# Sums of the spectral products moved to VectorE, rotations finished in their outputs, and the even half's inverse one step earlier

## The reference, cut to what matters

```python
x = x + 0.5 * ffn(layernorm(x))          # 4 x 1024 x 256, fp32
x = x + ssm(layernorm(x))
x = x + 0.5 * ffn(layernorm(x))          # the same weights

def ffn(x):                              # weights are ternary, each layer has its scales
    h = silu((x @ w1.T) * w1_s) * ((x @ w2.T) * w2_s)     # 256 -> 1024
    h = gelu((h @ h1.T) * h1_s)                            # 1024 -> 1024
    h = gelu((h @ h2.T) * h2_s)                            # 1024 -> 1024
    return (h @ w3.T) * w3_s                               # 1024 -> 256

def ssm(x):                              # per channel: convolution over the 1024 tokens with K(log_dt, A, C)
    y = irfft(rfft(x, 2048) * rfft(K, 2048), 2048)[:1024]
    return gelu(y) @ W.T + b
```

## Time and profile before

| what | value |
|---|---|
| median of 3 runs | 1566.58 us (1562.31, 1566.58, 1566.74) |
| the profiled execution's own time | 1557.19 us |
| its span, first to last instruction | 1555.4 us |
| PE busy | 1481.7 us, 95% |
| DVE busy | 1059.9 us, 68% |
| ACT busy | 523.1 us, 34% |
| POOL busy | 265.2 us, 17% |
| mean granted TensorE clock | 0.985 |

### The profile page before, as it was taken

How to read it: one execution, slowest core, us unless ns; L and a number is a source line. 1 busy time by engine, 2 the same in 40 slices (tenths; PEclk the granted TensorE clock), 3 DMA queues, 4 the chain that set the end, 5 groups by cost and what they waited for, 6 DMA issues and landing times.

```text
span 1555.4 us, 17475 instructions
## 1 busy us (share of the span) xinstructions
PE 1481.7 (95%) x6912; PEld 1194.5 (77%) x6912; DVE 1059.9 (68%) x1691; ACT 523.1 (34%) x743; POOL 265.2 (17%) x245
## 2 busy tenths in 40 slices
PE   7698979989999999999999999999999999999998
PEld 3477867777777777878778787687887878888887
DVE  6697577977758777786778867687477775344432
ACT  5334235444442331423324232232322323232231
POOL 0024563735500002001021010210102100000000
PEclk9899999999999999999999999999999999999999
DMA  8100000000010412103121031220212211000000
GB/s 303 53 1 28 27 15 14 28 14 14 28 38 28 144 46 68 62 17 122 41 78 58 11 122 41 68 68 33 74 41 68 68 38 42 27 14 28 28 1 14
DMA packets 52258, 78.24 MB, mean 50 GB/s; under 512 B 2768, under 2 KB 44752, under 8 KB 50896
## 3 DMA queue, kind: packets, MB, share of 16 engines
q1 hardware_dynamic: 52176, 77.12, 14.7%
HBM read 56.14 MB, written 20.97 MB: 50 GB/s over the span
## 4 chain that ended last, share of the span: by engine, by line
PE 76%; DVE 10%; issue 8%; ACT 3%; POOL 2%; DMA 1%; DVEq 0%; POOLq 0%; ACTq 0%
PE ps L1291 59%; PE ps L1333 7%; PE ps L1370 3%; PE ps L1423 2%; PE ps L1340 2%; DVE hid_a_lo L1215 1%; ACT L620 1%; DVE hid_a_hi L1213 1%; DVE table L886 1%; ACT ph L620 1%; DMA ks<-k_d 1%; PE ps L1364 1%; PE ps L1365 1%; DVE table L879 1%; DVE tt L1018 1%
## 5 line engine op out<-in xcount | busy, mean ns | idle before, releaser
L577 ACT ACTIVATE act_o<-ps,scales 128x512 f32<-128x512 f32 x384 | 264.8, 690 | 962.2 <-PE ps L1291 958.4
L1291 PE MATMUL ps<-hid_a_hi,h 128*128 128x512 f32 x1024 | 409.6, 400 | 6.3 <-DVE hid_a_lo L1206 6.1
L1291 PE MATMUL ps<-hid_b_hi,h 128*128 128x512 f32 x1024 | 404.9, 395 | 0.8 <-DVE hid_b_lo L1215 0.7
L1291 PE MATMUL ps<-hid_a_lo,h 128*128 128x512 f32 x1024 | 404.2, 395 | 0.0
L1291 PE MATMUL ps<-hid_b_lo,h 128*128 128x512 f32 x1024 | 401.6, 392 | 0.0
L1291 PEld LDWEIGHTS ps<-hid_a_hi,h 128*128 128x128 f32 x1024 | 194.6, 190 | 55.0 <-issue 7.5
L1291 PEld LDWEIGHTS ps<-hid_a_lo,h 128*128 128x128 f32 x1024 | 194.5, 190 | 43.4 <-issue 2.2
L1291 PEld LDWEIGHTS ps<-hid_b_hi,h 128*128 128x128 f32 x1024 | 192.5, 188 | 45.2 <-DVE hid_b_lo L1215 2.1
L1291 PEld LDWEIGHTS ps<-hid_b_lo,h 128*128 128x128 f32 x1024 | 192.5, 188 | 42.9 <-issue 1.2
L1291 PE MATMUL ps<-hid_b_hi,w 128*128 128x512 f32 x480 | 189.9, 396 | 2.4 <-DVE gz L1268 2.1
L1291 PE MATMUL ps<-hid_b_lo,w 128*128 128x512 f32 x480 | 188.9, 394 | 0.0
(11 more groups left out here) (235 smaller groups left out, 1707.5 us busy)
## 6 DMA issues: line engine op xcount, KB each, us to landing
ks<-k_d SPq DMA_DIRECT2D x32, 512.0 KB, 4.2
stages<-in_weights SPq DMA_DIRECT2D x8, 1024.0 KB, 7.7
gz<-in_x SPq DMA_DIRECT2D x8, 512.0 KB, 3.9
xin<-in_x SPq DMA_DIRECT2D x8, 512.0 KB, 3.9
x_d<-xin SPq DMA_DIRECT2D x8, 512.0 KB, 2.9
z_d<-xin SPq DMA_DIRECT2D x8, 512.0 KB, 2.9
k_d<-ks SPq DMA_DIRECT2D x8, 512.0 KB, 2.9
zb<-z_d SPq DMA_DIRECT2D x8, 512.0 KB, 5.6
```

Of the source, the lines that this page charges most:

```text
L577: A(act_o[:, k % ACT_SLOTS], bank(source), func, scale=scale).then_inc(s_act, 1)
L1291: last = MM(o, weight[:, k, cols].bitcast(dt), part[:, k].bitcast(dt), start=(k == 0 and i == 0), stop=(k == n - 1 and i == len(act_) - 1))
```

## The change

It has four parts.

1. The sum of each product's halves is done by DVE right behind the product, in `products`. All products go to `tt`, so each product and its sum wait for one another on DVE. POOL's `sums`, its two gathering additions and their semaphore s_y are gone; a new DVE function `gather_even` writes their results to `tt` and signals s_pre. PE's `inverse_even` reads them there.
2. `rotate` first writes the sine products into its two outputs and then finishes them in place, so it does not use `tt`. `rotate_quarter` now issues its two sine products itself, at its own step; `fold_third` issues two instructions fewer.
3. In first tiles the even products come at k = 14 to 17 and `gather_even` at k = 18, `rotate_odd` at k = 18 and 19 (was 14, 15), `inverse_even` on PE before step 20 (was 21), on ACT at k = 20, on DVE at k = 21 and 22. ACT's `copy_even` is at k = 14 (was 16), writes to fb and no longer waits for `rotate_odd`; `scale_even` does.
4. In first tiles norm1 is at k = 11, 12 (was 18, 19) and norm2 at k = 19, 20 (was 20, 21). On POOL in second tiles the two additions of the bias come before norm2's inverse root (were behind it).

```diff
     if first_of(T):
-        return 18, 19
+        return 11, 12
...
@@ norm2_at
+    if first_of(T):
+        return (19, 20) if T <= TILES else (-1, -1)
     return (20, 21) if 4 < T <= TILES else (-1, -1)
...
@@ POOL
-            def sums(c, i):
-                pool.wait_ge(s_prod, (c - 1) * 8 + i + 1)
-                t = product_home(i)
-                G.tensor_tensor(fb[:, spectrum_at(i)], t[:, 0:4:2], t[:, 1:4:2], ALU.add).then_inc(s_y, 1)
...
-                if first:
-                    for i in range(4):
-                        sums(first, i)
-                    inverse_root("first", T + 1)
-                    pool.wait_ge(s_y, (first - 1) * 8 + 4)
-                    G.tensor_tensor(zb[:, 0:2], fb[:, 4:6], fb[:, 6:8], ALU.add)
-                    G.tensor_tensor(zb[:, 2:4], fb[:, 4:6], fb[:, 6:8], ALU.subtract).then_inc(s_pre, 1)
-                    if norm2_at(T)[0] >= 0:
-                        inverse_root("second", T - 1)
-                elif second:
-                    for i in range(4, 8):
-                        sums(second, i)
+                if second:
                     inverse_root("first", T + 1)
                     pool.wait_ge(s_xc, 32 * second)
                     pool.wait_ge(s_wt, 32 * second)
-                    if norm2_at(T)[0] >= 0:
-                        inverse_root("second", T - 1)
                     for g in range(2):
                         half = wb[:, g * J:(g + 1) * J]
                         last = G.tensor_tensor(half, half, bias.unsqueeze(1).to_broadcast([P, J, D]), ALU.add)
                     last.then_inc(s_bias, 1)
+                    if norm2_at(T)[0] >= 0:
+                        inverse_root("second", T - 1)
+                elif first:
+                    inverse_root("first", T + 1)
+                    if norm2_at(T)[0] >= 0:
+                        inverse_root("second", T - 1)
...
@@ ACT
             def copy_even(c):
-                act.wait_ge(s_rb, c + 1)
                 act.wait_ge(s_ef, c + 1)
-                A(zb[:, 0:2], units(7), ACT.Copy).then_inc(s_cpe, 1)
+                A(fb[:, 4:6], units(7), ACT.Copy).then_inc(s_cpe, 1)
...
             def scale_even(c):
                 act.wait_ge(s_ei, c)
+                act.wait_ge(s_rb, c + 1)
...
-                if first and k == 16:
+                if first and k == 14:
                     copy_even(first)
-                if first and k == 21:
+                if first and k == 20:
                     scale_even(first)
...
@@ DVE
+            def rotate(out0, out1, x0, x1, c_, s_):
+
+                V.tensor_scalar(out0, x1, s_, None, ALU.mult)
+                mark(V.tensor_scalar(out1, x0, s_, None, ALU.mult))
+                marked()
+                V.scalar_tensor_tensor(out0, x0, c_, out0, ALU.mult, ALU.subtract)
+                return V.scalar_tensor_tensor(out1, x1, c_, out1, ALU.mult, ALU.add)
...
@@ products
-                if i >= 2:
-                    dve.wait_ge(s_y, n - 1)
                 marked()
...
-                V.tensor_tensor(t, x, k_, ALU.mult).then_inc(s_prod, 1)
+                V.tensor_tensor(tt.rearrange("p (h u) d -> p h (u d)", h=2), x, k_, ALU.mult).then_inc(s_prod, 1)
+                dve.wait_ge(s_prod, n + 1)
+                mark(V.tensor_tensor(fb[:, spectrum_at(i)], tt[:, 0:4:2], tt[:, 1:4:2], ALU.add))
+
+            def gather_even():
+                marked()
+                V.tensor_tensor(tt[:, 0:2], fb[:, 4:6], fb[:, 6:8], ALU.add)
+                V.tensor_tensor(tt[:, 2:4], fb[:, 4:6], fb[:, 6:8], ALU.subtract).then_inc(s_pre, 1)
...
                     if k in (14, 15):
-                        rotate_odd(k - 14)
+                        products(first, k - 14)
                     if k == 16:
-                        products(first, 0)
-                        products(first, 1)
-                    if k == 17:
                         spectrum_even(first)
                         products(first, 2)
-                    if k == 18:
+                    if k == 17:
                         products(first, 3)
+                    if k == 18:
+                        gather_even()
+                    if k in (18, 19):
+                        rotate_odd(k - 18)
+                    if k == 21:
+                        inverse_even(first)
                     if k == 22:
-                        inverse_even(first)
-                    if k == 23:
                         inverse_even_again(first)
...
@@ PE
-                whole(6, C4, zb[:, 0:2])
-                whole(7, S4, zb[:, 2:4], s_ei)
+                whole(6, C4, tt[:, 0:2])
+                whole(7, S4, tt[:, 2:4], s_ei)
...
-                if first and k == 21:
+                if first and k == 20:
                     inverse_even(first)
```

More of the change, by code:

```diff
@@ L255, in build @@
             "s_of", "s_cpo", "s_ab", "s_oi", "s_sco", "s_inv", "s_yt", "s_tr", "s_g", "s_pj", "s_x2", "s_x2st"))
-        s_prod, s_y, s_pre, s_preo, s_wt, s_xc, s_bias = (sem(n) for n in (
-            "s_prod", "s_y", "s_pre", "s_preo", "s_wt", "s_xc", "s_bias"))
+        s_prod, s_pre, s_preo, s_wt, s_xc, s_bias = (sem(n) for n in (
+            "s_prod", "s_pre", "s_preo", "s_wt", "s_xc", "s_bias"))
         s_mir, s_l1k, s_turn, s_kfin = (sem(n) for n in ("s_mir", "s_l1k", "s_turn", "s_kfin"))
@@ L956, in rotate_odd @@
                 marked()
-                V.tensor_scalar(tt[:, 0:2], x1, col(C_S4), None, ALU.mult)
-                mark(V.tensor_scalar(tt[:, 2:4], x0, col(C_S4), None, ALU.mult))
-                marked()
-                last = rotate(wb[:, 4 * h:4 * h + 2], wb[:, 4 * h + 2:4 * h + 4], x0, x1, col(C_C4))
+                last = rotate(wb[:, 4 * h:4 * h + 2], wb[:, 4 * h + 2:4 * h + 4], x0, x1, col(C_C4), col(C_S4))
                 if h:
@@ L990, in turn @@
                     dve.wait_ge(s_ef, 1)
+                    dve.wait_ge(s_rb, 1)
                 if i >= 2:
@@ L1039, in gather_odd @@
             def gather_odd(c):
-                dve.wait_ge(s_y, c * 8)
+                marked()
                 V.tensor_tensor(wb[:, 0:4], fb[:, 0:4], fb[:, 4:8], ALU.add)
@@ L1063, in unrotate @@
                 marked()
-                V.tensor_scalar(tt[:, 0:2], x, col(C_SA + j), None, ALU.mult)
-                mark(V.tensor_scalar(tt[:, 2:4], y, col(C_SA + j), None, ALU.mult))
-                marked()
-                last = rotate(fb[:, j:j + 7:6], fb[:, 2 + j:5 + j:2], y, x, col(C_CA + j))
+                last = rotate(fb[:, j:j + 7:6], fb[:, 2 + j:5 + j:2], y, x, col(C_CA + j), col(C_SA + j))
                 if j:
@@ L1130, in spectral @@
                     if k in (14, 15):
-                        rotate_odd(k - 14)
+                        products(first, k - 14)
                     if k == 16:
-                        products(first, 0)
-                        products(first, 1)
-                    if k == 17:
                         spectrum_even(first)
                         products(first, 2)
+                    if k == 17:
+                        products(first, 3)
                     if k == 18:
-                        products(first, 3)
+                        gather_even()
[3 more added lines that the diff above has]
+                        inverse_even(first)
                     if k == 22:
-                        inverse_even(first)
-                    if k == 23:
                         inverse_even_again(first)
```

25 lines of the change are left out of this document (5 added, 20 removed).

## The result

The changed kernel takes 1535.62 us, the median of 4 runs (1533.72 to 1538.41); the kernel before, run beside it, 1564.44 (4 runs, 1558.42 to 1566.74). The ratio is 0.9824, 95% interval 0.9802 to 0.9847. The forecast was 1546.0 with a range of 1540 to 1554: the sign and the mechanism came true, the size is outside the range. The medians lie 28.8 us apart, the profiled executions less: 1555.4 us of span before, 1534.3 after, so 21.1 us, and the forecast said 20.6.

What follows compares the result with a forecast made beforehand. PE, busy 95% of the span, was taken as the bound; its wait and slow clock at the even inverse cost 21.2 us. Minus about 0.15 x 4 this gave 20.6, so 1566.6 - 20.6 = 1546.0 us, range 1540 to 1554.

Steps and rivals of the forecast that it cites:

- The wait and the clock behind it: PE at the even inverse of four first tiles: 12.7 us of wait, 8.5 of slow clock and restart.
- the ceiling: Most the change could win: wait and slow clock at the even inverse over four first tiles, 21.2 us.
- The first tile: First tiles were to last 92.3 to 93.0 us instead of 97.6, at clock 1.00.
- the part kept back: Remaining PE wait for s_pre at the even inverse, 0 to 0.3 us per first tile; about 0.15 x 4 deducted.
- DVE's chain: First tiles, k = 14 to 18: product-and-sum pairs of 1.9 us, s_pre at 791.1, 0.1 to 0.3 us of slack.
- The zeros: Parts costed at 0: rotate_odd's move, norm1 at k = 11 and 12, second tiles, bias order, T = 4.
- A: Rival: s_pre comes 0.5 to 2 us late at the even inverse; gain 11 to 17, 1550 to 1556 us; chance 0.11.
- B: Rival: an equal wait takes its place at scale_even or layer_three; no gain seen, 1562 to 1570 us; chance 0.06.
- C: Rival: late tap load for product 2 or 3 holds DVE's queue; slower, 1574 us at 8 us late; chance 0.04.
- the last move of the sum: The 20.6 us saving was taken from the median, 1566.6 to 1546.0, instead of the profiled execution, 1557.2 to 1536.6.

Runs made afterwards that it cites:

- second profile of before: The kernel before, unchanged, profiled again: 1559.88 us (span 1558.1), one run.
- the repeat of the changed kernel: The changed kernel as it is, run again beside the kernel before on chip 0: 1535.1 us (5 runs), ratio 0.9821.

## Why the prediction was wrong in size

By its own steps, the mechanism held. What failed is the baseline from which the saving was taken, and the saving itself was sized too small: 20.6 us, where T = 5 to 12 gave 23.5.
- **The wait and the clock behind it** are gone, 47.1 us of ACT's idle became 4 x 6.42 = 25.7: 21.4 us, where the ceiling was 21.2 and the forecast 20.6. The 0.15 us per tile kept back for a late s_pre was not needed: gather_even's last addition ends at 784.71, PE starts the inverse at 785.09.
- **The first tile** T = 7 came to 92.16 us; 92.3 to 93.0 was named, again without the part kept back.
- **DVE's chain** came true within 0.05 us at each point, with the measured cost of the wait between product and sum. The sum starts 0.03 us after its product's end (778.67 against 777.41 + 1.23), a split that waits for neither 0.08 before the sum's end, so the wait costs 0.11 us. The Trainium skill, "VectorE: DVE Perf Modes", section "The DRAIN you can't avoid", says that the semaphore costs nothing extra. The trace disagrees by that 0.11 us, and the measurement decides.
- **The zeros** (rotate_odd, norm1, second tiles, bias order, T = 4) were right within what the runs can tell: no new wait of PE stands in T = 4 to 12, the four second tiles take 376.0 us together against 375.8 before, and the moves of the norms and of the bias order were undone for 1 us at most. rotate_odd's move and T = 4 were not undone by themselves.
- **Rivals**: A's 0.5 to 2 us of lateness didn't come about. What it would have cost was measured: a wait of 1.0 us costs 1.2, the lower end of the 1 to 2.5 that it named, with no loss of clock. B's covers held. For C, DVE waits twice for the taps in the profile after, 1.2 and 1.0 us, in T = 10 and 12 and not in a first tile; it did not before, and PE does not wait for it.

**What failed is the last move of the sum**: "The median is 9.4 us above that execution, a spread that no row explains; I take the saving from the median", with a range that ended at 1540. The profiled execution of before was one at the faster length. Two of the three runs behind the median, 1566.58 and 1566.74, are of the slower by their time, while all four runs of the result have a clock of 0.988 or more, the faster. So the saving was taken from one length and compared with the other. Taken from the profiled execution, 1557.2 - 20.6 = 1536.6 would have come within 1.0 us of the result, in part by luck, since the saving was too small as well. From 1566.58 to 1535.62 is 31.0 us. Of it:
- 20.6 as forecast, and 0.6 more because nothing of the part kept back was needed.
- 2.3 omitted: eight tiles, T = 5 to 12, take 769.7 us before (mean of three profiles) and 746.3 after (mean of four), 23.5 less. Of the 2.3, 0.5 is that the idle behind the inverse fell by 21.7 on average, over the ceiling of 21.2 that one profile gave. 1.2 is the last step of the first tiles, 13.9 us from ACT's start to the next tile's before and 13.6 after, of which I know no cause. 0.6 has no place of its own.
- 3.5 because the three runs shown gave a median over the 1563.1 that 57 runs give; 2.6 because the four runs of the result lie under the 1538.2 of 20 runs.
- 1.4 is the rest of the pooled gain (24.9). It may be no more than the mix of chips and lengths in the two medians, since within one length on one chip the gain is 22.7 to 24.4 us.

The pace of the hidden steps, which the prediction had at "up to 0.07 longer" in the other first tiles, explains 0.3 us of this at most. In the first profile of before, T = 5, 9 and 11 run the steps between the two transforms at 3.73 us, as here from 584.02 to 587.75, and the first profile after runs them at 3.66. But the second profile of before has 3.66 in all four tiles, as here from 584.82 to 588.48 in T = 5, and the repeat of the changed kernel has 3.73 in T = 7. The pace differs from execution to execution in both kernels.

```profile
584.02 0.69 ACT L577 ACTIVATE act_o<-ps,scales 128x512 f32<-128x512 f32 x1 [3.04 <-PE ps L1291]
587.75 0.69 ACT L577 ACTIVATE act_o<-ps,scales 128x512 f32<-128x512 f32 x1 [3.04 <-PE ps L1291]
```

```profile
584.82 0.69 ACT L577 ACTIVATE act_o<-ps,scales 128x512 f32<-128x512 f32 x1 [2.97 <-PE ps L1291]
588.48 0.69 ACT L577 ACTIVATE act_o<-ps,scales 128x512 f32<-128x512 f32 x1 [2.98 <-PE ps L1291]
```

What was in hand spoke against that last move. The profiled execution was one of the same kernel's and lay 9 us under the median, so executions had to differ by that much where nothing was changed; a range for a median of a few runs must hold one such step on either side, as must a baseline of three. And even the pooled 1538.2 lies under 1540, so the range was also too tight for the part of the saving that was omitted.

Open: what puts an execution on one level or the other; why hidden steps run at 3.73 in some stretches and 3.66 in others; the 1.2 us at the end of the first tiles. What a late tap load in a first tile would cost (C) was not tried, since none came late there.

## What to carry to other kernels

Before work is moved between engines to close a wait, see whether the waiting engine can ask one step later: here one number gave all of the gain but about 1 us. A gap of 3 us in PE's stream cost 1.7 times its length here, a gap of 1 us only 0.3 us more than itself, so partial closing pays more than in proportion. When the profiled execution and the median differ by more than the effect's uncertainty, find the stretch of untouched code that holds the difference before the saving is applied to either. And before a difference of two profiles is given a cause, look at a second profile of each kernel: the pace of the steps seemed to be part of the gain until one was read.

## What the runs showed of the hardware

The loss behind a gap on PE is not in proportion to it. Behind waits of 0.96 and 1.24 us the clock is 1.00 in the 5 us that follow and the loss is 0.3 us; behind four waits of 2.4 us the clock is 0.66 and the loss 1.9 us three times, 1.00 and 0.3 us once; behind waits of 3.1 to 3.4 us the clock is 0.50 to 0.71 and the loss 1.7 to 3.3 us, with the same six products of matrices in each case. So a gap of 2.4 us can be enough to bring the clock down. And unchanged code in the same kernel ran at a mean clock of 0.98 or 0.94 over 210 us from one execution to the next, and T = 3 ended 4.9 us later in the second.

A wait of DVE for its own last operation costs 0.11 us (from 0.08 us before its end to 0.03 behind it). Four 128x256 operations of DVE took 5.48 us beside two additions of POOL and 1.38 without them; when only the order was put back in the changed kernel, they took 5.47.
